# Short norm coefficients, silu(z) by tile, z copied first, and the recurrent part without its loop

## What is computed

```
h    = rmsnorm(layernorm(x)) ;  proj = h @ w_in        # z, x, B, C, dt
x    = silu(conv4(x)) ;  dt = softplus(dt @ w_dt + b_dt)
for each chunk: M = exp(masked differences of cumsum(dt * A))
    y     = (M * (C B^T)) x + exp(cumsum) C state      # 8 heads of 32, state 64
    state = total_decay * state + (M[last] * x)^T B
y    = rmsnorm((y + D * x) * silu(z))
x2   = x + layernorm(layernorm(x) + y @ w_out)
out  = x2 + layernorm(experts(layernorm(x2)))          # top 2 of 8 experts, relu
```

## Time and profile before

| | |
|---|---|
| median of 3 runs | 1142.01 us (1137.75 to 1142.52) |
| profiled execution | 1139.66 us, its span 1137.9 us |
| PE, PE weight loads, DVE, ACT, POOL busy | 91, 76, 82, 57, 54% of the span |
| mean granted clock of PE | 0.967 |
| first decays (L752) of group 0, of group 2, of group 14 | 39.56, 110.6, 592.25 us |
| first expert work on PE | 668.09 us |
| chain that ended last, by engine | PE 55%, DVE 11%, issue 11%, POOL 10%, ACT 7% |

### The profile page before, as it was taken

The page is one execution under the profiler, slowest core; times in us unless marked ns, Lnnn a source line. Parts: engine busy times, 40 slices in busy tenths (PEclk is TensorE's granted clock), DMA queues, the critical chain, the costliest instruction groups (busy, mean ns, idle before and its releaser), DMA issues.

```text
span 1137.9 us, 29655 instructions
## 1 busy us (share of the span) xinstructions
PE 1036.1 (91%) x9060; PEld 869.2 (76%) x9060; DVE 936.5 (82%) x2590; ACT 653.9 (57%) x1237; POOL 612.8 (54%) x873
## 2 busy tenths in 40 slices
PE   3899998998998998988999877999999999999996
PEld 2677776776776776776778666898988888888885
DVE  5668895886786787787778766999999999999997
ACT  4778776775876776675787432444444444444442
POOL 7345563554555555455554542555555555555654
PEclk9999998998998998998999988999999999999998
DMA  6000000000000000000000300000000000000000
GB/s 181 4 3 4 3 4 5 1 4 5 3 2 5 3 2 4 4 3 3 4 3 3 97 1 1 10 11 10 9 9 9 9 9 9 9 9 9 10 11 18
DMA packets 19586, 14.41 MB, mean 13 GB/s; under 512 B 4361, under 2 KB 16929, under 8 KB 19489
## 3 DMA queue, kind: packets, MB, share of 16 engines
q1 hardware_dynamic: 19488, 13.02, 4.2%
HBM read 7.77 MB, written 4.19 MB: 11 GB/s over the span
## 4 chain that ended last, share of the span: by engine, by line
PE 55%; DVE 11%; issue 11%; POOL 10%; ACT 7%; DMA 2%; SPq 1%; POOLq 1%; DVEq 1%; ACTq 0%
PE bank L1591 16%; PE bank L1564 4%; PE bank L1565 4%; PE bank L768 4%; PE bank L1566 4%; PE bank L840 2%; PE bank L752 2%; PE bank L560 2%; DVE moe_acc L1640 2%; PE bank L562 2%; DVE moe_h L1442 2%; PE bank L561 2%; PE bank L754 2%; POOL ln_scale L497 2%; PE bank L550 2%
## 5 line engine op out<-in xcount | busy, mean ns | idle before, releaser
L1575 ACT ACTIVATE moe_hid<-bank,moe_b 128x512 f32<-128x512 f32 x256 | 167.2, 688 | 172.6 <-PE bank L1566 172.2
L1591 PEld LDWEIGHTS bank<-moe_w,moe_hid 128*128 128x128 f32 x2048 | 249.5, 193 | 21.4 <-ACT moe_hid L1575 5.8
L1591 PE MATMUL bank<-moe_w,moe_hid 128*128 128x128 f32 x2048 | 252.4, 277 | 5.3 <-DVE moe_acc L1640 2.7
L1640 DVE SCALAR_TENSOR_TENSOR moe_acc<-bank,moe_scores,moe_acc 128x128 f32<-128x128 f32 x448 | 125.6, 341 | 22.3 <-PE bank L1591 20.1
L852 ACT ACTIVATE m<-bank 128x512 f32<-128x512 f32 x128 | 70.1, 595 | 88.9 <-PE bank L754 88.9
L932 DVE TENSOR_TENSOR mg<-bank,m 128x512 f32<-128x512 f32 x128 | 82.4, 685 | 43.2 <-PE bank L768 42.7
L560 PE MATMUL bank<-thi,whi 128*128 128x512 f32 x224 | 105.9, 473 | 10.1 <-ACT bt L601 3.8
L1564 PE MATMUL bank<-moe_t_hi,moe_w_hi 128*128 128x512 f32 x256 | 113.9, 445 | 0.0
L1617 POOL TENSOR_TENSOR moe_b_mix<-moe_b_mix 128x512 f32<-128x512 f32 x80 | 107.5, 1344 | 10.2
L923 POOL TENSOR_TENSOR y<-y,zt 128x256 f32<-128x256 f32 x64 | 46.8, 731 | 118.5 <-DVE y L947 117.9
L1565 PE MATMUL bank<-moe_t_lo,moe_w_hi 128*128 128x512 f32 x256 | 102.9, 402 | 0.0
(11 more groups left out here) (178 smaller groups left out, 2530.8 us busy)
## 6 DMA issues: line engine op xcount, KB each, us to landing
out_dram<-moe_outb SPq DMA_DIRECT2D x16, 256.0 KB, 2.3
parts<-csplit SPq DMA_DIRECT2D x128, 4.0 KB
rows<-csplit SPq DMA_DIRECT2D x128, 4.0 KB
moe_w<-in_L_ffn_W_dram SPq DMA_DIRECT2D x1, 1024.0 KB, 5.5
m<-in_L_attn_w_in_proj_dram SPq DMA_DIRECT2D x1, 772.0 KB
xall<-in_L_attn_hidden_dram SPq DMA_DIRECT2D x2, 256.0 KB, 3.6
moe_b<-in_L_ffn_b_dram SPq DMA_DIRECT2D x1, 512.0 KB, 8.1
mg<-n_L_attn_w_out_proj_dram SPq DMA_DIRECT2D x1, 128.0 KB, 2.4
```

Of the source, the lines that this page charges most:

```text
L1575: SE.activation(hid[:, e % 2, n, :], up_banks[k % 4][:], ACT.Relu, bias=b1[:, k:k + 1]).then_inc(hid_ready.sem, 1)
L1591: mm = PE.matmul(bank[:, col(i)], hid[:, e % 2, n, col(i)], w2[:, e, n, :], start=n == 0, stop=n == FB - 1, skip_group_check=True)
L1640: DVE.scalar_tensor_tensor(out=acc[:, par, i, :], in0=y, scalar=s, in1=acc[:, par, i, :], op0=ALU.mult, op1=ALU.add).then_inc(acc_step.sem, 1)
```

## The change

Five edits, all but the last in the recurrent part.

- `pool_norm`: six instructions in place of nine, with three waits in place of nine. From var it forms var·(1 + eps') + eps·eps' and var + eps side by side and takes both to the power −0.5 in one instruction of 8 columns; −mean is formed beside them; one product gives the bias, one copy the scale s1.
- silu(z): the product of the whole group in tile 0 (`pool_silu_z`) is gone; `pool_gate` multiplies the tile's own 128 tokens ahead of its gate. zsig has two buffers, the second in the half of m that becomes free because m now has one: `act_decays` waits for mg and xw of tile t − 1 where it waited for t − 2.
- In tile 2, ACT copies z out of its banks ahead of the first exponent of the x sigmoid.
- The loops of `over_sequences` and of the row copies become Python loops: all 16 groups are straight programs.
- SP no longer waits for silu(z) of the last group before it loads the experts' weights.

```diff
-    m = m_flat[:].rearrange("p (b h l) -> p b h l", b=2, h=NH)
+    m = m_flat[:, 0:NH * P].rearrange("p (h l) -> p h l", h=NH)
...
-    zsig = sb("zsig", [P, NB, GT])
+    zsig = [sb("zsig0", [P, NB, GT]), m_flat[:, NH * P:].rearrange("p (n l) -> p n l", n=NB)]
...
-        PL.tensor_scalar(lnt[:, 0, :], var, LN_EPS, None, ALU.add).then_inc(coef_step.sem, 1)
-        pl.wait_ge(coef_step.sem, coef_step.of(f, 1))
-        apart(pl, f)
-        PL.tensor_tensor(rs, lnt[:, 0, :], neghalf[:], ALU.pow).then_inc(coef_step.sem, 1)
...
+        PL.tensor_scalar(lnt[:, 2, :], var, 1.0 + RMS_EPS, LN_EPS * RMS_EPS, ALU.mult, ALU.add
+                         ).then_inc(coef_step.sem, 1)
+        PL.tensor_scalar(lnt[:, 3, :], var, LN_EPS, None, ALU.add).then_inc(coef_step.sem, 1)
+        PL.tensor_scalar(lnt[:, 5, :], mean, -1.0, None, ALU.mult).then_inc(coef_step.sem, 1)
         pl.wait_ge(coef_step.sem, coef_step.of(f, 2))
         apart(pl, f)
+        PL.tensor_tensor(lnt[:, 0:2, :].rearrange("p k t -> p (k t)"), lnt[:, 2:4, :].rearrange("p k t -> p (k t)"),
+                         neghalf2[:], ALU.pow).then_inc(coef_step.sem, 1)
         pl.wait_ge(coef_step.sem, coef_step.of(f, 4))
         apart(pl, f)
+        PL.tensor_tensor(lnt[:, 4, :], lnt[:, 5, :], lnt[:, 0, :], ALU.mult).then_inc(coef_step.sem, 1)
+        PL.tensor_copy(rs, lnt[:, 1, :]).then_inc(coef_step.sem, 1)
...
-            if due(f - 1):
-                act.wait_ge(zt_ready.sem, zt_ready.of(f - 1))
-            SE.activation(zsig[:], zt[par][:], ACT.Exp, scale=-1.0).then_inc(zsig_step.sem, 1)
+            if due(f - 2):
+                act.wait_ge(zt_ready.sem, zt_ready.of((f - 2) * TG + TG - 1))
+            SE.activation(zsig[par][:], zt[par][:], ACT.Exp, scale=-1.0).then_inc(zsig_step.sem, 1)
...
-            if hf == 0 and due(t - 2):
-
-                act.wait_ge(mg_ready.sem, mg_ready.of(t - 2))
-                act.wait_ge(xw_ready.sem, xw_ready.of(t - 2))
+            if hf == 0 and due(t - 1):
+
+                act.wait_ge(mg_ready.sem, mg_ready.of(t - 1))
+                act.wait_ge(xw_ready.sem, xw_ready.of(t - 1))
...
         if i == 0:
-            pl.wait_ge(zt_ready.sem, zt_ready.of(g))
+            pl.wait_ge(zsig_step.sem, zsig_step.of(g))
+        apart(pl, t)
+        PL.tensor_tensor(zt[par][:, :, col(i)], zsig[par][:, :, col(i)], zt[par][:, :, col(i)], ALU.mult
+                         ).then_inc(zt_ready.sem, 1)
+        pl.wait_ge(zt_ready.sem, zt_ready.of(t))
         pl.wait_ge(y_step.sem, y_step.of(t))
...
-            pool_silu_z(pl, g, par)
...
-        with eng.Fori(1, BATCH - 1) as b:
+        for b in range(1, BATCH - 1):
             for u in range(GB):
                 run(eng, body, b, u, False)
...
-        with sp.Fori(1, BATCH) as b:
+        for b in range(1, BATCH):
             for u in range(GB):
                 row_copies(sp, b, u)
...
-        sp.wait_ge(zt_ready.sem, zt_ready.of(G_LAST))
```

More of the change, by code:

```diff
@@ L134, in attention @@
     zeros = keep("zeros", [P, 1])
-    neghalf = keep("neghalf", [P, TG])
+    neghalf2 = keep("neghalf", [P, 2 * TG])
+    neghalf = neghalf2[:, 0:TG]
     rank = keep("rank", [P, TG, NE])
@@ L526, in act_h @@
             x = xall[:, dyn(f * TG + i, 1), :].rearrange("p o d -> p (o d)")
-            SE.activation(h[:, par, i, :], x, ACT.Identity, scale=lnt[:, 0, i:i + 1], bias=lnt[:, 1, i:i + 1]
+            SE.activation(h[:, par, i, :], x, ACT.Identity, scale=lnt[:, 0, i:i + 1], bias=lnt[:, 4, i:i + 1]
                           ).then_inc(h_ready.sem, 1)
@@ L638, in act_z_sigmoid @@
             act.wait_ge(z_ready.sem, z_ready.of(f))
-            if due(f - 1):
-                act.wait_ge(zt_ready.sem, zt_ready.of(f - 1))
-            SE.activation(zsig[:], zt[par][:], ACT.Exp, scale=-1.0).then_inc(zsig_step.sem, 1)
+            if due(f - 2):
+                act.wait_ge(zt_ready.sem, zt_ready.of((f - 2) * TG + TG - 1))
+            SE.activation(zsig[par][:], zt[par][:], ACT.Exp, scale=-1.0).then_inc(zsig_step.sem, 1)
         if step == 1:
             act.wait_ge(zheld.sem, zheld.of(f))
-            SE.activation(zsig[:], zsig[:], ACT.Ln, bias=1.0).then_inc(zsig_step.sem, 1)
+            SE.activation(zsig[par][:], zsig[par][:], ACT.Ln, bias=1.0).then_inc(zsig_step.sem, 1)
         if step == 2:
             act.wait_ge(zsig_step.sem, zsig_step.of(f, 2))
-            SE.activation(zsig[:], zsig[:], ACT.Exp, scale=-1.0).then_inc(zsig_step.sem, 1)
+            SE.activation(zsig[par][:], zsig[par][:], ACT.Exp, scale=-1.0).then_inc(zsig_step.sem, 1)
     def dve_conv(dve, f, par, steps):
@@ L717, in dve_front @@
             dve.wait_ge(zsig_step.sem, zsig_step.of(f, 1))
-            DVE.tensor_scalar(zsig[:], zsig[:], EXP_MAX, None, ALU.min).then_inc(zheld.sem, 1)
+            DVE.tensor_scalar(zsig[par][:], zsig[par][:], EXP_MAX, None, ALU.min).then_inc(zheld.sem, 1)
         if key == "xt":
@@ L847, in act_decays @@
             act.wait_ge(dd_done.sem, dd_done.of(t, hf + 1))
-            if hf == 0 and due(t - 2):
-                act.wait_ge(mg_ready.sem, mg_ready.of(t - 2))
-                act.wait_ge(xw_ready.sem, xw_ready.of(t - 2))
-            SE.activation(m[:, tp, hf * HH:(hf + 1) * HH, :], banks[2 + hf][:].rearrange("p (h l) -> p h l", l=P),
+            if hf == 0 and due(t - 1):
+                act.wait_ge(mg_ready.sem, mg_ready.of(t - 1))
+                act.wait_ge(xw_ready.sem, xw_ready.of(t - 1))
+            SE.activation(m[:, hf * HH:(hf + 1) * HH, :], banks[2 + hf][:].rearrange("p (h l) -> p h l", l=P),
                           ACT.Exp).then_inc(m_ready.sem, 1)
@@ L1074, in act_body @@
             act_softplus(act, f, 0)
-        if f is not None and i == 2:
-            act_x_sigmoid(act, f, fu, 0)
         if f is not None and i == 3:
@@ L1081, in act_body @@
                 act_front(act, f, fu, fr, key)
+        if f is not None and i == 2:
+            act_x_sigmoid(act, f, fu, 0)
         if not begin:
```

37 lines of the change are left out of this document (8 added, 29 removed).

## The result

The changed kernel takes 1103.59 us (median of 4 runs, 1100.6 to 1106.13), the kernel before 1142.09 (4 runs, 1137.75 to 1142.52): a ratio of 0.967, 95% interval 0.963 to 0.971. The profiled execution took 1101.95 us, its span 1099.9. Forecast were 1085 us and a range of 1076 to 1099: the direction was right, the time lies 4.6 us above the range.

A forecast was written before the change was run, and what follows sets the result against it. TensorE, never free, plus whatever stops it was taken to bound the recurrent part. Savings of 50.8 (straight groups) + 0.5 (z first) + 3.0 (start) + 0.4 (into the experts) = 54.7 us from 1139.66 gave 1085 us, range 1076 to 1099.

The forecast's parts named there:

- Straight programs, 12 × 35.9 = 430.8 us: Recurrent groups 2 to 13: written out straight they take 35.9 us each instead of 481.65 in all; 50.8 us go.
- Norm coefficients: POOL, tile 1: norm shrinks from 6.57 to 3.8 us, silu product adds 0.8, so the gate starts at about 248.3.
- the wait goes: ACT's 1.79 us wait for POOL's gate before its square disappears; about 0.5 us stays with a power of 2.1.
- Silu by tile, z first, m: Recurrent tiles: silu split in four, counted nothing; z copied first, 0.5 us in all; one m buffer, cost 0.
- Start, −3.0: Start of the kernel: group 0's norm on POOL shortens ACT's waits; 3.0 us saved, between 1.5 and 5.3.
- Into the experts, −0.4: Before the experts: weight loads no longer wait for the last group's silu(z); 0.4 us saved.
- The experts' part: Experts' loop: no change counted; rival that its moved loop refetches at six jumps, 6.0 us each: 1121 us, chance 0.02.
- The upper bound: Whole kernel: least saving of group and start, 1139.66 − 45.1 = 1094.5 us, widened to 1099 for run spread and row copies.
- Late row copies: Rival, recurrent groups: row copies make every group 1 us late, 12 more: 1097 to 1098 us; chance 0.08.
- Only the jumps go: Rival, groups 2 to 13: the body's 1.6 us a group stay, twelve take 450 us: 1105 us; chance 0.07.
- Late packets of straight code: Rival, straight groups: PE's 36 instruction packets each come late, 2.7 us a stop, 97 us: 1182 us; chance 0.03.
- DVE held by POOL: Rival, recurrent tiles 1 to 3: four silu products hold DVE 0.74 us each, 31 us in all: 1116 us; chance 0.04.

The follow-up runs named there:

- the kernel with 64 waits: Changed kernel with 64 already fulfilled waits, each on a no-op, at the start of DVE's program: 1083.37 us, ratio 0.950.
- that with 77: Changed kernel with 77 already fulfilled waits, each on a no-op, at the start of DVE's program: 1101.48 us, ratio 0.964.
- the all-straight form: Changed kernel with the experts' turns also written out straight on every engine, SP too: 1118.24 us, ratio 0.979.

## Why the prediction was off, step by step

The step that failed is the one on the experts' part; the two smaller misses are the norm's price and the way into the experts. In the order of the sum:

- **Straight programs, 12 × 35.9 = 430.8 us.** Right: 429.7. By themselves they bring 481.65 − 433.8 = 47.9 us, and the other edits 4.1 on top. But in a loop the norm alone brings 13.5: the two overlap, because both take away the delay of tile 2. Tile 2 takes 10.86 us before, 10.0 in straight programs with the old norm, 9.79 in the loop with the new norm, and 9.62 with both. The prediction didn't say this; it took the length of straight groups as one number, and so didn't count it twice.
- **Norm coefficients.** The mechanism is right, its price was too low. Rows of POOL in tile 1 of group 5 and of ACT behind it, to be read against the earlier trace rows:

```profile
228.32 0.62 POOL L495 TENSOR_SCALAR lnt<-mv 128x4 f32<-128x4 f32 x1
...
230.27 1.66 POOL L501 TENSOR_TENSOR lnt<-lnt,neghalf 128x8 f32<-128x8 f32 x1
232.01 0.20 POOL L505 TENSOR_TENSOR lnt<-lnt 128x4 f32<-128x4 f32 x1
232.15 0.72 POOL L506 COPY ln_scale<-lnt 128x4 f32<-128x4 f32 x1
232.84 1.24 POOL L903 TENSOR_TENSOR zt<-m,zt 128x256 f32<-128x256 f32 x1
234.15 1.06 POOL L910 TENSOR_TENSOR y<-y,zt 128x256 f32<-128x256 f32 x1
...
235.25 0.42 ACT L858 ACTIVATE ysq<-y 128x256 f32<-128x256 f32 x1 [1.27 <-POOL y L910]
```

  The power of 8 columns takes 1.66 us (taken 1.4, bounds 1.04 and 2.1), the norm 232.15 + 0.72 − 228.32 = 4.55 instead of 3.8, the product 1.24 instead of 0.8 and the gate 1.06. The gate starts 5.83 us behind the norm's start, where the prediction had 4.6 and the kernel before 6.57. So "the wait goes" is wrong: 1.27 of 1.79 us stay, in every group (15.3 us in twelve). Tile 2 came to 9.63 us all the same: PE's only wait for ACT in groups 2 to 13 is the one for h, 2.5 us in all, so PE does not wait for what stands behind that square. The prediction's time for tile 2 was right without its reason.
- **Silu by tile, z first, m.** Right: nothing was counted for the first and the last, and ACT's exponents of the decays wait only for PE. PE's wait for the copy of z, 8.0 us in the loop before, is gone; with the loops put back the three edits together brought 1.4 us and not more.
- **Start, −3.0.** Measured −3.1. The run with the norm alone gives −2.7, so the cause is the one named. The first decimal is luck: in the traces of the other kernels with all five edits the first decays come at 36.2 to 38.0 us.
- **Into the experts, −0.4.** Wrong, by 2.3 us. The loads are issued 42.5 us behind the start of group 14 (before 43.4), but DVE can go on only 54.5 us behind it, before 54.3 (compare):

```profile
579.13 0.40 SPq L1747 DMA_DIRECT2D moe_w<-in_L_ffn_W_dram  x1
...
591.12 0.87 DVE L1400 BATCH_NORM_STATS2 moe_st<-xall 128x6 f32<-128x128 f32 x4 [4.80 <-DMA moe_b<-in_L_ffn_b_dram]
```

  The last load's landing sets this time, 9.4 us from issue instead of 8.1. DVE comes to it 1.6 us earlier than before and only waits longer. That makes 0.2 of the 1.9 us. The rest lies behind it, in PE's clock; windows up to the experts' first transposes, before and after:

```profile
646.50:656.50 10.00, 6.83 (x76) 5.18 (x75) 9.81 (x33) 4.20 (x7) 5.43 (x8) 1.00 0.01 2
591.00:602.80 11.80, 9.66 (x70) 7.74 (x70) 11.52 (x35) 4.33 (x7) 5.82 (x8) 0.57 0.01 1
```

  While DVE waits, PE runs out of work: it stands 3.21 us for DVE's mg, where it stood 1.38 before. Behind that the granted clock falls to 0.50, and the 16 score products of the tile (L768, now L751) take 2.08 us instead of 1.16. The traces of the other kernels with all five edits agree. Where the clock of the last 12 us was 0.57, the stretch took 65.5 to 66.4 us, where it was 0.72, 64.2 to 64.7, and where it was 0.86 or 1.00, 63.6 to 64.0; the kernel with 64 waits is among the second, that with 77 among the third. What makes the clock fall in one of them and not in another was not tested. The 1.9 us are no fixed price of the change.
- **The experts' part.** The step that failed. The prediction set it at no change because its code is unchanged, and gave 0.02 to its loop being fetched anew. That is what happened, on DVE and not on PE, at 3.1 us for each of five jumps back (the prediction counted six) and not 6.0: 15.7 us in all. The argument took PE's rows for the limit and never asked for the other engines: the earlier trace rows has q8 alone, PE's queue. By the rule that the runs gave, the kernel before had its loop 7 behind an edge, with room for 3 more instructions, and a loop that is moved without regard to it lands on a good place 11 times in 128. Even without the rule, a loop that is kept at one place and moved by 955 instructions deserved far more than 0.02. With 1085 + 15.7 + 2.3 = 1103 the rest of the sum holds, and with the loop on a good place the changed kernel gives 1081 to 1083.4 us.
- **The upper bound.** It has two slips that decide nothing: 45.1 us is 43.6 + 1.5 and leaves out the 0.5 and the 0.4 of the sum, and 0.5 us of wait in each of twelve groups are 6 us, not 5.
- **The rivals.** Late row copies: PE waited 1.0 us for them in all of groups 2 to 13; it fell. Only the jumps go: fell, since straight programs alone give 36.1 us a group. Late packets of straight code: fell; no matmul of PE waited on "issue" in groups 2 to 13, and the granted clock was 1.00 from 50 to 590 us. DVE held by POOL: perhaps a little in the recurrent part, where DVE is busy 29.34 us in group 1 and was 27.91, but PE's work covers it; the same effect is large in the experts' part, where straight code takes the no-ops away.

## To carry to other kernels

A change that makes a program longer or shorter moves every loop behind it; look in the trace for instruction packets and for stops at the jump on each engine, not only on the one that bounds, and try the loop a few dozen instructions further on before judging the change. Here that was worth 20 us, half of what the change itself brought. Where a loop is written out straight, look at what its no-ops did beside their purpose: on POOL they were worth 50 us in the all-straight form. Here it was enough to write out DVE's loop alone (1083 us) or to move it (1081 to 1083), and the gaps on POOL were worth another 11 us. The version that came of it (all straight, with the no-ops on POOL in the experts' part) takes 1068 us, 6.4% less than the kernel before.

## What was not expected of the hardware

- At the ten places seen here, a loop of DVE was kept where it lay in three successive 8 KB pieces of its program (384 instructions), six times, and not where it reached into a fourth, four times. One instruction over, and each turn brings 5 packets and each jump back a stop of 2.9 to 4.2 us.
- Of PE's loops, that of 812 instructions was kept at both places (3 or 4 packets in 350 us), that of 1,609 in the recurrent part was not (8 packets of 16 KB a turn). No run moved one of them across an edge, so PE's limit is open.
- POOL's power takes 1.03 to 1.39 us for 4 columns and 1.66 for 8, between 0.07 and 0.16 us for each further column; a plain product of 1,024 columns takes 2.37 us.
- A no-op between POOL's products, 0.07 us each, takes DVE's L1427 from 1.20 to 0.37 us at the median. That the gap lets DVE in is read from these rows and from the 50 us; the port itself isn't in the trace.
